# Self-attention scores from one folded weight Wq·Wkᵀ, with the two biases as a column shift and a row term

## The reference

```python
q = x @ Wq + bq
k = x @ Wk + bk
v = x @ Wv + bv
scale = jnp.asarray(EMB, x.dtype) ** 0.5                 # EMB = 512
scores = jnp.einsum('btd,bsd->bts', q, k) / scale
scores = jnp.where(causal, scores, NEG_INF)
m = jnp.max(scores, axis=(-2, -1), keepdims=True)
e = jnp.exp(scores - m)
w = e / jnp.sum(e, axis=(-2, -1), keepdims=True)        # over the whole 32x32 square
return jnp.einsum('bts,bsd->btd', w, v)
```

## Time and profile before

| | us |
|---|---|
| median of the runs shown | 2917.51 |
| the three runs | 2917.20, 2917.51, 2921.46 |
| span of the profiled execution | 2917.1 |
| cross-attention blocks | 1919.4 |
| round 0, to the first power of round 1 | 88.8 |
| the 14 rounds after it, together | 830.8 |
| the rest of round 15, and round 16 | 78.1 |
| PE / DVE / ACT / POOL busy, share of the span | 96% / 57% / 43% / 27% |

### The profile page before, as it was taken

The page is one execution under the profiler, slowest core; times in us unless marked ns, Lnnn a source line. Parts: engine busy times, 40 slices in busy tenths (PEclk is TensorE's granted clock), DMA queues, the critical chain, the costliest instruction groups (busy, mean ns, idle before and its releaser), DMA issues. The chain is left out here.

```text
span 2917.1 us, 54809 instructions
## 1 busy us (share of the span) xinstructions
PE 2794.1 (96%) x18492; PEld 1704.0 (58%) x18492; DVE 1668.3 (57%) x3620; ACT 1267.4 (43%) x2954; POOL 776.4 (27%) x1530
## 2 busy tenths in 40 slices
PE   7999999999999999999999999957999999899999
PEld 4455555555555555555555555534666666566666
DVE  7555555555555555555555555556665666656664
ACT  4344444444444444444444444423433443344444
POOL 2233333333333333333333333211111111111110
PEclk9999999999999999999999999978999999999999
DMA  4211111111111111111111111022000000000000
GB/s 143 83 56 55 62 41 40 40 48 41 40 40 48 41 40 40 48 41 40 40 48 41 40 40 48 13 84 66 15 30 15 15 14 22 22 14 14 14 23 15
DMA packets 65959, 118.49 MB, mean 41 GB/s; under 512 B 12016, under 2 KB 32496, under 8 KB 65392
## 3 DMA queue, kind: packets, MB, share of 16 engines
q1 hardware_dynamic: 65904, 117.76, 12.4%
HBM read 109.06 MB, written 8.65 MB: 40 GB/s over the span
## 5 line engine op out<-in xcount | busy, mean ns | idle before, releaser
L656 DVE SCALAR_TENSOR_TENSOR kT_lo<-psum,kT_hi 128x512 f16<-128x512 f32 x256 | 177.1, 692 | 440.2 <-ACT kT_hi L587 440.2
L591 ACT ACTIVATE v_hi<-psum 128x512 f16<-128x512 f32 x256 | 152.8, 597 | 552.7 <-PE psum L746 552.7
L746 PE MATMUL psum<-c_hi,xWk_hi 128*128 128x512 f16 x1024 | 388.1, 379 | 2.3 <-PEq L136 2.3
L746 PE MATMUL psum<-xWv_hi,c_hi 128*128 128x512 f16 x1024 | 388.3, 379 | 0.0
L746 PE MATMUL psum<-xWv_lo,c_hi 128*128 128x512 f16 x1024 | 388.1, 379 | 0.0
L746 PE MATMUL psum<-xWv_hi,c_lo 128*128 128x512 f16 x1024 | 388.1, 379 | 0.0
L746 PE MATMUL psum<-c_lo,xWk_hi 128*128 128x512 f16 x1024 | 388.1, 379 | 0.0
L746 PE MATMUL psum<-c_hi,xWk_lo 128*128 128x512 f16 x1024 | 388.1, 379 | 0.0
L118 POOL TENSOR_TENSOR c_lo<-ctx_raw,c_hi 128x1024 f16<-128x1024 f32 x128 | 272.5, 2129 | 429.8 <-ACT c_hi L583 419.2
L662 DVE SCALAR_TENSOR_TENSOR v_lo<-psum,v_hi 128x512 f16<-128x512 f32 x256 | 177.1, 692 | 360.4 <-ACT v_hi L591 360.4
L597 ACT ACTIVATE e<-psum,neg_max 128x257 f32<-128x257 f32 x512 | 236.3, 474 | 281.9 <-DVE neg_max L651 281.9
(11 more groups left out here) (195 smaller groups left out, 5986.9 us busy)
## 6 DMA issues: line engine op xcount, KB each, us to landing
ctx_raw<-in_ctx_main SPq DMA_DIRECT2D x128, 512.0 KB, 3.3
xs<-in_x SPq DMA_DIRECT2D x8, 1024.0 KB, 5.5
v_rep<-v_last_rows SPq DMA_DIRECT2D x512, 16.0 KB, 2.3
xb<-in_x SPq DMA_DIRECT2D x16, 512.0 KB, 3.3
out<-res_out SPq DMA_DIRECT2D x32, 256.0 KB, 2.0
ffn_raw<-in_w_t SPq DMA_DIRECT2D x11, 512.0 KB, 3.4
late_raw<-in_late_w SPq DMA_DIRECT2D x4, 1024.0 KB, 4.7
res<-in_w_t SPq DMA_DIRECT2D x5, 512.0 KB, 3.5
```

The costliest lines, as they stand in the source:

```text
L591: nc.scalar.mul(v_hi[u][:, t, :], v_bank(t), W_UNSCALE).then_inc(v_hi_done, 1)
L656: nc.vector.scalar_tensor_tensor(out=kT_lo[r][:, m, :, 0:S], in0=k_bank(m), scalar=W_UNSCALE, in1=kT_hi[r][:, m, :, 0:S], op0=ALU.mult, op ...
L746: mm = nc.tensor.matmul(bank, a, b, start=(n == 0), stop=(n == len(steps) - 1))
```

## The change

Scores of a pair of tokens are (x Wq + bq)·(y Wk + bk), which is x·M·yᵀ with M = Wq Wkᵀ, plus bq Wkᵀ·y, plus x·(Wq bk), plus bq·bk. The changed kernel multiplies M once, at the start of `token_stages`, and keeps it in the place of sWq. Each front then projects x by M alone: two banks instead of four. The term in y becomes a shift of the projection's columns (`shift_col`, in the place of the bias column at ACT's move from PSUM); the term in x is one number per row, which DVE computes from `xn` and `row_w` (`row_terms`) and adds to the mask together with the constant. The scores are then taken against `x2T_hi`, `x2T_lo`, instead of the split k.

To multiply M, the weights are turned by matmuls against an identity (`turn`), moved out of PSUM and split again (ACT in its `fold_weights`, DVE in `turn_weights`), multiplied (PE's `fold_weights`, 48 matmuls of 512 columns, then 12 of 512 and 60 of one column for the bias terms) and split once more (ACT, and DVE in `fold_products`). ACT's `fold_weights` and DVE's `turn_weights` stand ahead of `rounds`; PE's `turn` too; PE's `fold_weights` stands in round 0 ahead of the transposes, DVE's `fold_products` in round 0 behind the split of x2T.

```diff
-qk_hi = sb_in(ctx, "qk_hi", [P, 2 * KC, GROUP], F16)
-qk_lo = sb_in(ctx, "qk_lo", [P, 2 * KC, GROUP], F16)
+qk_hi = sb_in(ctx, "qk_hi", [P, KC, GROUP], F16)
+qk_lo = sb_in(ctx, "qk_lo", [P, KC, GROUP], F16)
...
-late = {name: (late_hi[:, w], late_lo[:, w]) for w, name in enumerate(("xWo", "sWq", "sWk", "sWv"))}
+late = {name: (late_hi[:, w], late_lo[:, w]) for w, name in ((0, "xWo"), (1, "sM"), (3, "sWv"))}
...
-QK_BANK = (2, 3, 0, 1)
+QK_BANK = (2, 3)
+def turn_bank(i):
+    return psum[:, i % 4, :]
+def turned(late_part, i):
+    return late_part[:, 1 + i // KC, i % KC, :]
...
         if front:
-            if isinstance(n, int) and n == 0:
-                eng.wait_ge(s["consts_landed"], 16 * 6)
-            for r in range(4):
-                eng.wait_ge(s["qk_ps"], 4 * n + r + 1)
-                past(eng, s["qk_lo_done"], 4 * n + r - 1)
+            for r in range(2):
+                eng.wait_ge(s["qk_ps"], 2 * n + r + 1)
+                past(eng, s["qk_lo_done"], 2 * n + r - 1)
                 for c in range(2):
                     last = nc.scalar.activation(
-                        qk[r % 2][:, c, :], chunks(g_bank(QK_BANK[r]), 2)[:, c, :], ACT.Identity,
-                        bias=bqk_col[:, 2 * r + c:2 * r + c + 1], scale=W_UNSCALE)
+                        qk[r][:, c, :], chunks(g_bank(QK_BANK[r]), 2)[:, c, :], ACT.Identity,
+                        bias=shift_col[:, 2 * r + c:2 * r + c + 1], scale=W_UNSCALE)
                 last.then_inc(s["qk_done"], 1)
...
             eng.wait_ge(alpha1_done, 1)
+    def fold_weights():
+        eng.wait_ge(s["consts_landed"], 16 * 6)
+        nc.scalar.mul(bias_hi[:, :], bqk_col[:, :], W_SCALE).then_inc(s["bias_hi_done"], 1)
+        for i in range(2 * KC):
+            eng.wait_ge(s["turn_ps"], KC * (i // KC + 1))
+            nc.scalar.copy(turned(late_hi, i), turn_bank(i)).then_inc(s["turn_hi_done"], 1)
+        eng.wait_ge(s["fold_vec_ps"], 1)
+        nc.scalar.mul(row_w[:, :], g_bank(0), SCALE * W_UNSCALE * W_UNSCALE)
+        nc.scalar.mul(shift_col[:, :], g_bank(1)[:, 0:KC], W_UNSCALE * W_UNSCALE)
+        nc.scalar.mul(const_col[:, :], g_bank(1)[:, KC:KC + 1],
+                      SCALE * W_UNSCALE * W_UNSCALE).then_inc(s["fold_vec_done"], 1)
+        for m in range(KC):
+            nc.scalar.mul(late_hi[:, 1, m, :], turn_bank(m), W_UNSCALE).then_inc(s["fold_hi_done"], 1)
+        eng.wait_ge(s["fold_vec_done"], 1)
     nc.scalar.copy(at_hi[:, :, :], heads_hi[:, :, 0:GROUP]).then_inc(s["at_done"], 1)
+    fold_weights()
     rounds(eng, one)
...
     def projections(n):
-        for r in range(4):
+        for r in range(2):
             cols = slice(2 * r, 2 * r + 2)
-            dve.wait_ge(s["qk_done"], 4 * n + r + 1)
-            nc.vector.tensor_copy(qk_hi[:, cols, :], qk[r % 2][:, :, :]).then_inc(s["qk_hi_done"], 1)
-            dve.wait_ge(s["qk_hi_done"], 4 * n + r + 1)
-            nc.vector.tensor_tensor(qk_lo[:, cols, :], qk[r % 2][:, :, :], qk_hi[:, cols, :],
+            dve.wait_ge(s["qk_done"], 2 * n + r + 1)
+            nc.vector.tensor_copy(qk_hi[:, cols, :], qk[r][:, :, :]).then_inc(s["qk_hi_done"], 1)
+            dve.wait_ge(s["qk_hi_done"], 2 * n + r + 1)
+            nc.vector.tensor_tensor(qk_lo[:, cols, :], qk[r][:, :, :], qk_hi[:, cols, :],
                                     ALU.subtract).then_inc(s["qk_lo_done"], 1)
+    def row_terms(n):
+        for t in range(T):
+            dve.wait_ge(s["norm2_done"], T * n + t + 1)
+            past(dve, s["row_term_done"], T * n + t)
+            nc.vector.tensor_tensor_reduce(
+                out=val[:, :], in0=xn[:, t, :], in1=row_w[:, :], op0=ALU.mult, op1=ALU.add,
+                scale=1.0, scalar=0.0, accum_out=row_term[:, t:t + 1]).then_inc(s["row_term_done"], 1)
+        dve.wait_ge(s["row_term_done"], T * (n + 1))
+        nc.vector.tensor_tensor(mask_row[:, :, :], row_term[:, :].unsqueeze(2).to_broadcast([P, T, BT]),
+                                mask[:, :].unsqueeze(1).to_broadcast([P, T, BT]),
+                                ALU.add).then_inc(s["mask_row_done"], 1)
...
         dve.wait_ge(s["sc_ps"], n + 1)
+        dve.wait_ge(s["mask_row_done"], n + 1)
         for b in range(BPT):
...
                 out=sc[rows, :, :], in0=sc_bank[rows, :, BT * b:BT * b + BT], scalar=SCALE,
-                in1=mask[rows, :].unsqueeze(1).to_broadcast([BT, T, BT]), op0=ALU.mult,
+                in1=mask_row[rows, :, :], op0=ALU.mult,
                 op1=ALU.add).then_inc(s["sc_done"], 1)
...
             low_T(s["x2T_hi_done"], x2T_hi, x2T_lo, s["x2T_lo_done"], n)
+            if isinstance(n, int) and n == 0:
+                fold_products()
+            row_terms(n)
         F(5)
...
         if front:
-            if isinstance(n, int) and n == 0:
-                dve.wait_ge(s["mask_done"], BPT)
-                dve.wait_ge(s["consts_landed"], 16 * 6)
             maxima(n)
...
             dve.wait_ge(mag_done, 2 * NW)
+    def turn_weights():
+        for i in range(2 * KC):
+            dve.wait_ge(s["turn_hi_done"], i + 1)
+            nc.vector.tensor_tensor(turned(late_lo, i), turn_bank(i), turned(late_hi, i),
+                                    ALU.subtract).then_inc(s["turn_lo_done"], 1)
+    def fold_products():
+        for m in range(KC):
+            dve.wait_ge(s["fold_hi_done"], m + 1)
+            nc.vector.scalar_tensor_tensor(out=late_lo[:, 1, m, :], in0=turn_bank(m), scalar=W_UNSCALE,
+                                           in1=late_hi[:, 1, m, :], op0=ALU.mult,
+                                           op1=ALU.subtract).then_inc(s["fold_lo_done"], 1)
+        dve.wait_ge(s["mask_done"], BPT)
+        dve.wait_ge(s["fold_vec_done"], 1)
+        nc.vector.tensor_scalar(mask[:, :], mask[:, :], const_col[:, :], None,
+                                ALU.add).then_inc(s["mask_const_done"], 1)
+        dve.wait_ge(s["mask_const_done"], 1)
     nc.vector.tensor_copy(at_lo[:, :, :], heads_lo[:, :, 0:GROUP]).then_inc(s["at_done"], 1)
+    nc.vector.tensor_copy(ident_h[:, :], ident[:, :]).then_inc(s["ident_h_done"], 1)
+    dve.wait_ge(s["bias_hi_done"], 1)
+    nc.vector.scalar_tensor_tensor(out=bias_lo[:, :], in0=bqk_col[:, :], scalar=W_SCALE,
+                                   in1=bias_hi[:, :], op0=ALU.mult,
+                                   op1=ALU.subtract).then_inc(s["bias_lo_done"], 1)
+    dve.wait_ge(s["bias_lo_done"], 1)
+    for src, dst in ((bias_hi, bk_rep_hi), (bias_lo, bk_rep_lo)):
+        nc.vector.tensor_copy(dst[:, :, :], src[:, KC:].unsqueeze(2).to_broadcast([P, KC, P])
+                              ).then_inc(s["bias_rep_done"], 1)
+    turn_weights()
     rounds(dve, one)
...
         mm.then_inc(added, 1)
+    def turn(w):
+        for c in range(KC):
+            if w == 2:
+                pe.wait_ge(s["turn_lo_done"], c + 1)
+            for k in range(KC):
+                cols = slice(k * P, (k + 1) * P)
+                mm = run(turn_bank(c)[:, cols], [(part[:, w, k, c * P:(c + 1) * P], ident_h[:, :])
+                                                 for part in (late_hi, late_lo)])
+            mm.then_inc(s["turn_ps"], 1)
+    def fold_weights():
+        pe.wait_ge(s["turn_lo_done"], 2 * KC)
+        for m in range(KC):
+            cols = slice(m * P, (m + 1) * P)
+            mm = run(turn_bank(m), [(q[:, 1, e, cols], k[:, 2, e, :]) for e in range(KC)
+                                    for q, k in passes(late_hi, late_lo, late_hi, late_lo)])
+        mm.then_inc(s["fold_ps"], 1)
+        pe.wait_ge(s["bias_rep_done"], 2)
+        run(g_bank(0), [(b[:, e, :], q[:, 1, e, :]) for e in range(KC)
+                        for b, q in passes(bk_rep_hi, bk_rep_lo, late_hi, late_lo)])
+        for m in range(KC):
+            cols = slice(m * P, (m + 1) * P)
+            run(g_bank(1)[:, m:m + 1], [(k[:, 2, e, cols], b[:, e:e + 1]) for e in range(KC)
+                                        for k, b in passes(late_hi, late_lo, bias_hi, bias_lo)])
+        run(g_bank(1)[:, KC:KC + 1], [(r[:, e, :], b[:, e:e + 1]) for e in range(KC)
+                                      for r, b in passes(bk_rep_hi, bk_rep_lo, bias_hi, bias_lo)]
+            ).then_inc(s["fold_vec_ps"], 1)
...
         if front:
+            if isinstance(n, int) and n == 0:
+                fold_weights()
+                pe.wait_ge(s["fold_vec_done"], 1)
             transposes(n, s["norm2_done"], s["t2_ps"])
...
             pe.wait_ge(s["x2T_lo_done"], T * (n + 1))
-            for r in range(4):
-                hi, lo = late["sWq" if r < 2 else "sWk"]
+            if isinstance(n, int) and n == 0:
+                pe.wait_ge(s["fold_lo_done"], KC)
+            for r in range(2):
+                hi, lo = late["sM"]
                 for c in range(2):
-                    m = 2 * (r % 2) + c
+                    m = 2 * r + c
                     mm = run(chunks(g_bank(QK_BANK[r]), 2)[:, c, :],
...
         if front:
```

(30 more changed lines are left out.)

## The result

The changed kernel takes **2849.05 us** in the median (2847.67 to 2850.64), the kernel before 2918.82 us in the runs beside it: a ratio of 0.9761, 95% interval 0.9747 to 0.9774. The forecast was 2853.4 us in a range of 2838 to 2877. The profiled execution has a span of 2847.1 us against 2917.1.

What follows compares the result with a forecast made beforehand. PE was taken to bound the rounds, standing about 4 us in each; 2917.1 − 78.6 (rounds) + 22.4 (round 0) − 7.9 (clock) = 2853.0 on the span, 0.4 more for the median: 2853.4 us, range 2838 to 2877.

Steps and rivals of the forecast that it cites:

- Rounds 1 to 15: PE's projections: 48 of 96 matmuls fewer at 0.109 us, 5.24 us a round, 78.6 us less in all.
- The row term: DVE's two products with sums ahead of the splits of q: 2.0 us a round, hidden, counted as 0.
- The room: DVE's time from 2076.24 until the row term would make the scores wait: 7.3 us.
- Round 0: Turning, folding and row term stand on the path at the start: 22.4 us later, ends 17 and 45.
- the 60 one-column matmuls: PE's bias terms in round 0's fold: 0.056 us each as in the scores, 3.4 us; ends 0 and 13.2.
- The hold of POOL on the remainder of the biases: Round 0: DVE's remainder of the biases falls into POOL's add and ends with it, at 1931.0.
- The clock: 14 holes of PE: one in three loses nothing, others 2.16 us; 20.2 in all, 7.9 us less than now.
- the rivals: Holes each lose 2.97, 2874.8 us, 0.10 (mirror 2833.2, 0.08); fold costs double, 2876.4, 0.10; row term delays scores, past 2923, 0.03.
- narrower range: The sum's own range, with 17 to 30 for round 0 and half of the clock's ends: 2840 to 2866 us.
- the third: DVE's row term becomes the wait ahead of the scores, paid 15 times: slower, past 2923 us; chance 0.03.
- the second: Round 0's fold costs double, wide matmuls at half clock, one-column matmuls not overlapping: 2876.4 us; chance 0.10.
- the hole itself: PE waits 3.58 us a round for `gelu_lo` on DVE ahead of the transposes, away from what the change shortens.

Runs made afterwards that it cites:

- the half move: Changed kernel with only POOL's addition of the output bias moved behind the row term, its copies of heads left in place: 2801.68 us, ratio 0.9593.

## Why the prediction was right, step by step

**Rounds 1 to 15: −78.6 forecast, −78.5 measured.** 57.34 less 52.10 is the 5.24 of 48 × 0.109; 14 rounds and the end make 73.36 + 5.18. The step that carried it was to see in the earlier trace rows that DVE had time to spare where PE lost work.

**The row term: 2.0 us forecast and counted at nothing; 1.8 measured, and nothing.** The product with its sum takes 0.69, what two sources took in the earlier trace rows, and the accumulator's read 0.08 where ACT's 0.19 was taken. By the half-rate rule of the Trainium skill (Vector Engine (DVE) Microarchitecture Reference, "Points that are easy to get wrong") each product would by estimate have taken 0.53 us more; the trace does not show it, 0.69 us for two float32 sources in SBUF. The page states the rule for the form S2S2D2_STT, and the trace names this instruction CUSTOM_DVE_ANT_0, so whether the rule means it stays open. The room was forecast at 7.3 us, to the scores. The limit is the right one, and the size a little high for the rounds at full clock, 6.3. I had named the `gelu_lo` of the second layer's chunk 5 and not asked when PE needs it: its room, 7.9 us, is so near that the eightfold row term made PE wait there first.

**Round 0: +22.4 forecast, +18.75 measured.** The pieces are those forecast, and from the fold on each was a little smaller:

```
                                       forecast    after
remainder of the biases ends            1931.0    1931.86
second residual ends                    1942.9    1943.53
PE done with the fold                   1958.8    1957.2
projections start                       1967.0    1964.30
magnitudes start on DVE                 1969.1    1966.05
fourth magnitude                        1977.0    1973.67
```

The mis-sized term is the 60 one-column matmuls: 3.4 us forecast, from the 0.056 of the scores; they start 0.025 us apart (1955.59 to 1957.07), 1.5 us in all. Here the estimate by the Trainium skill's floor of 25 ns between matmuls (TensorE: Matmul & The Clock Gate, "Wait — 56ns, not 53.3ns?") would have been 1.9 us nearer, and the trace agrees with that floor. From the transposes to the projections it took 6.25 instead of 7.1 us, and the mask and row term 1.75 instead of 2.1. The hold of POOL on the remainder of the biases was forecast with its end; that it could be avoided by another order was not seen.

**The clock: −7.9 forecast, −10.8 measured.** Five of 14 holes lost nothing (one in three was taken), nine lost 1.92 on average (2.16 was taken). The estimate was in the right place for a fair reason, since the kinds of outcome stayed, but it could not be more than a guess at frequencies, and that it came so near is in part luck. The reading that the loss does not hang on the length of a hole was drawn from holes of one length; the half move's, of 1.44 us, cost nothing.

**The sum.** −78.6 + 22.4 − 7.9 = −64.1 was forecast and −70.0 came: 3.65 from round 0 and 2.9 from the clock, less the 0.6 by which this execution came late to round 0. The median of the runs missed by less, 4.35 us, because it lies 1.95 us over this span and not the 0.4 that the prediction added. None of the rivals showed: the fold ran at full clock (60 matmuls of 512 columns 0.216 apart, from 1942.63 on), the holes that cost the most were two of 14, and the row term stayed hidden.

Some of the prediction's own figures do not follow from its terms, without bearing on the result. Its narrower range, 2840 to 2866, would be 2838 to 2872 with the ends that it names added up. With a room of 7.3 us the row term eats the gain from 11.6 us on and reaches 2923 at 11.9, not 11.4 and 11.8. And the rival that prices too short a cover is the third, not the second.

What was missing is a question the prediction did not put: what the hole itself is made of. It was read as a fixed part of the round, 3.58 us behind a `gelu_lo`, when the row ahead of it, the norm at 2.42 us beside POOL, already told: in the same trace round 15, without POOL's work there, had the norm at 1.00 us and no hole.

## What to carry to other kernels

When a change takes work off the bounding engine, the gain is the pitch of the removed instructions times the rounds, provided the engine that gets the new work stands idle at that place and all that is queued behind the new work, not just what it feeds, is in time. A one-time cost at the start is paid in full where the engines have nothing else to do; look first for a wait in it that another order avoids, here 9 of some 23 us. And a hole that a change leaves alone is worth asking about: compare the instruction that ends it with its twin elsewhere in the round (2.42 against 1.00 us), and look at what POOL does beside it.

## What the runs showed of the hardware

POOL's instructions hold some of DVE's and not others. Beside a POOL copy or addition, the norm with one SBUF source took 2.42 instead of 1.00 us for its two tiles, a product of two SBUF sources 1.32 instead of 0.69, a cast from SBUF 1.35 instead of 0.43; the split of x2T, with one source in PSUM and one in SBUF, kept its 0.69 a tile under the copies (1.29 for two at 2177.95, while POOL copied from 2177.92 to 2179.94). That fits what the Trainium skill says (SBUF — State Buffer, "Who interferes with whom"): DVE and POOL share a pair of ports as an exclusive lock, which a DVE instruction needs with two SBUF inputs (against a POOL instruction that reads SBUF) or as a copy, cast or `tensor_scalar` in a two-port mode, and not with one SBUF input otherwise. Each of these DVE instructions ends 0.3 to 0.5 us behind POOL's, as it would if it had waited for such a lock; no run here measured the lock by itself, nor shows which mode these instructions ran in. POOL was held as well: its second copy took 1.23 us beside the norm and 1.04 where it was moved away from it.

The clock's loss goes by the hole: 3.58 us of standing lost nothing in five rounds, about 1.7 us in seven and 2.7 in two, of the same kernel with the same instructions; 1.44 us lost nothing in 14. The kernel without the row term and the one with four times of it have the same lengths of rounds 1 to 14 to 0.03 us, and another order of them than the changed kernel. What decides between the outcomes of a 3.58-us hole was not settled.
